# ScalarE's copy of the first row transform, placed ahead of two squares instead of behind them and a state part

## The reference

```python
x = x + _L0_conv_ref(_gn(x))      # DCT along both axes of every channel
x = x + _L1_conv_ref(_gn(x), ...) # six Euler steps of a small network
```

## Time and profile before

| what | value |
|---|---|
| median of 3 runs | 3459.21 us (3457.57 to 3469.12) |
| the profiled execution: its own time | 3467.75 us |
| its span in the profile | 3465.9 us, mean granted clock 0.935 |
| TensorE matmul (PE) busy | 3005.5 us, 87% of the span |
| TensorE weight load (PEld) busy | 2541.5 us, 73% |
| VectorE (DVE) busy | 2717.9 us, 78% |
| ScalarE (ACT) busy | 2440.3 us, 70% |
| GpSimd (POOL) busy | 875.2 us, 25% |
| DMA | 217.56 MB, mean 63 GB/s |

### The profile page before, as it was taken

The page is one execution under the profiler, slowest core; times in us unless marked ns, Lnnn a source line. Parts: engine busy times, 40 slices in busy tenths (PEclk is TensorE's granted clock), DMA queues, the critical chain, the costliest instruction groups (busy, mean ns, idle before and its releaser), DMA issues.

```text
span 3465.9 us, 148163 instructions
## 1 busy us (share of the span) xinstructions
PE 3005.5 (87%) x61684; PEld 2541.5 (73%) x61684; DVE 2717.9 (78%) x6273; ACT 2440.3 (70%) x3819; POOL 875.2 (25%) x1293
## 2 busy tenths in 40 slices
PE   3699988999889998899988999899988999888984
PEld 2578776777777787678767877777777777777873
DVE  6688876888868887788877888688886888768883
ACT  0377777677776777777776777777777767787774
POOL 3134311432123221223212331133311332111111
PEclk8799998999999999899999999999998999999997
DMA  3400033112231330322304213221133113131014
GB/s 84 89 22 22 25 55 96 49 49 80 37 96 49 91 72 4 96 77 69 68 18 112 66 49 68 59 87 49 50 67 96 49 49 92 25 95 59 31 49 112
DMA packets 370208, 217.56 MB, mean 63 GB/s; under 512 B 354544, under 2 KB 354912, under 8 KB 367456
## 3 DMA queue, kind: packets, MB, share of 16 engines
q1 hardware_dynamic: 369504, 207.64, 24.2%
HBM read 104.85 MB, written 77.07 MB: 52 GB/s over the span
## 4 chain that ended last, share of the span: by engine, by line
ACT 23%; PE 23%; issue 20%; DVE 20%; POOL 6%; DMA 3%; SPq 3%; DVEq 1%; POOLq 0%; ACTq 0%
PE cps L1482 16%; ACT z L714 8%; ACT z L682 6%; DVE y L1118 3%; PE sps L1597 3%; POOL m L562 3%; ACT unread_z L702 3%; PE tps L1588 3%; SPq L449 2%; DVE ha L1114 2%; DVE bnt L1144 2%; ACT hb L713 2%; ACT ha L713 2%; DVE hb L1114 2%; DMA y<-xa 2%
## 5 line engine op out<-in xcount | busy, mean ns | idle before, releaser
L1482 PE MATMUL cps<-ha,w 64*64 64x392 f16 (+1 forms) x27648 | 1418.8, 347 | 126.3 <-ACT z L682 75.4
L1482 PEld LDWEIGHTS cps<-ha,w 64*64 64x64 f16 x27648 | 1081.1, 110 | 332.0 <-issue 159.0
L1482 PE MATMUL cps<-hb,w 64*64 64x392 f16 x27648 | 1278.5, 334 | 20.8 <-issue 14.1
L1482 PEld LDWEIGHTS cps<-hb,w 64*64 64x64 f16 x27648 | 1091.7, 108 | 114.3 <-issue 25.9
L682 ACT ACTIVATE z<-cps,bias_now 128x784 f32<-128x784 f32 (+2 forms) x1056 | 759.1, 737 | 582.3 <-PE cps L1482 578.4
L519 POOL TENSOR_TENSOR small<-small,half 128x1 f32<-128x1 f32 x304 | 168.1, 553 | 1646.0 <-DVE small L1018 1008.4
L1114 DVE TENSOR_TENSOR ha<-z,ha 128x784 f16<-128x784 f32 (+2 forms) x384 | 385.0, 1003 | 150.4 <-ACT z L714 145.6
L1114 DVE TENSOR_TENSOR hb<-z,hb 128x784 f16<-128x784 f32 (+2 forms) x384 | 374.8, 976 | 86.6 <-ACT z L714 77.8
L1144 DVE BATCH_NORM_STATS2 bnt<-z 128x6 f32<-128x392 f32 (+1 forms) x768 | 385.8, 547 | 56.1 <-ACT z L682 55.7
L1118 DVE SCALAR_TENSOR_TENSOR y<-z,small,y 128x784 f32<-128x784 f32 (+2 forms) x384 | 396.4, 1035 | 0.1
L714 ACT ACTIVATE z<-z,small 128x784 f32<-128x784 f32 (+2 forms) x384 | 396.1, 1031 | 0.0
(11 more groups left out here) (161 smaller groups left out, 2650.9 us busy)
## 6 DMA issues: line engine op xcount, KB each, us to landing
xa<-x_dram SPq DMA_DIRECT2D x128, 196.0 KB, 5.1
y<-xa SPq DMA_DIRECT2D x16, 1568.0 KB, 7.6
y_dram<-y SPq DMA_DIRECT2D x128, 196.0 KB, 4.7
x_dram<-x1s SPq DMA_DIRECT2D x30, 784.0 KB, 6.0
fin<-y_dram SPq DMA_DIRECT2D x30, 784.0 KB, 7.5
xs<-in_x_dram SPq DMA_DIRECT2D x116, 196.0 KB, 4.5
fin<-x_dram SPq DMA_DIRECT2D x28, 784.0 KB, 5.7
out_dram<-fin SPq DMA_DIRECT2D x28, 784.0 KB, 3.6
```

The lines of the kernel that those rows point to most:

```text
L1482: return pe.matmul(dst, w[hin * 64:(hin + 1) * 64, kx, a, wl, :], src[:, :, 0:NA], start=(what == "X" and n == 0), stop=(what == "Y" and n ...
```

## The change

The copy of batch 0 moves up in ScalarE's order: from behind two squares and a state part to directly behind the fourth evacuation of phase 2. The helper that issues it is defined earlier so that it can be called there. Nothing else differs.

```diff
--- before
+++ after
@@ -756,6 +756,10 @@
                 def posted(what, slot):
                     return NPOST * (posts_before(g, s, kind) + POSTS[kind].index((what, slot)) + 1)
 
+                def copied(b):
+                    if kind == MID:
+                        batch_copy(b, NBATCH * hn + b, tps)
+
                 def final_state(slot, k):
 
                     act.wait_ge(yup_done, yup + NP * slot + 2 * k + 2)
@@ -817,6 +821,7 @@
                 squares(1, 1, c, sq + 5)
                 evacuate(1, 1, s, 2, 2, c)
                 evacuate(1, 1, s, 2, 3, c)
+                copied(0)
                 squares(1, 2, c, sq + 6)
                 squares(1, 3, c, sq + 7)
                 if kind == FIVE:
@@ -833,11 +838,6 @@
 
                 c = conv_at(g, s, 3)
 
-                def copied(b):
-                    if kind == MID:
-                        batch_copy(b, NBATCH * hn + b, tps)
-
-                copied(0)
                 copied(1)
                 evacuate(0, 0, s, 3, 0, c)
                 copied(2)
```

## The result

The changed kernel takes 3374.25 us (median of 4 runs, 3368.23 to 3376.15) against 3459.44 us (4 runs, 3457.57 to 3469.12). The ratio is 0.975, 95% interval 0.9733 to 0.9766. The profiled execution has a span of 3374.3 us and a mean granted clock of 0.952 (before: 3465.9 and 0.935).

The account below looks back on a forecast made before the run. TensorE was taken to bound the 28 MID steps (busy 62.03 of 66.23 us), its stalls being winnable. From the profiled 3467.75 us, 35 for waits and 56.4 for clock falls came off: 3376 us, range 3360 to 3433.

Parts of the forecast that it names:

- (a): Moved copy on ScalarE: row transform ends 0.63 us before the evacuation does (0.4 to 0.8 over steps), new wait 0.
- The slower rival: ScalarE stalls 2.4 us at the copy behind late rows at low clock; 3510 us, chance 0.06.
- (b): TensorE's stall for the copy removed: batch 1's rows start 2.40 us earlier.
- (d): Slot 1's statistics matmul next waits for VectorE's fourth product: 1.68 of 2.40 us left, new idle time 0.7 us.
- (c): ScalarE's squares and state part, queued behind the copy, each come later by its slot, 0.42 us.
- (e): VectorE's last split waits for the state part; L1062 reads statistics 0.9 us earlier; TensorE waits 0.1 for batch 0's `x1s`.
- (f): Second stall, batch 2's columns on `x1s`: grows from 1.05 to 1.4 us; step gains 1.25 us, 35 us over 28.
- (g): TensorE's clock falls behind the removed stall vanish, 16 long (3.04 us) and 5 short (1.55 us): 56.4 us.
- the clock's term: The 56.4 us forecast from TensorE no longer falling to 1.2 GHz behind the stall in MID steps.
- that of the waits: The 35 us forecast from shorter waiting, 28 MID steps at 1.25 us each.
- Rival 1: Two or three remaining idle times still bring TensorE's clock down; 3433 us, 3405 with half the falls, chance 0.18.

Follow-up runs that it names:

- the filled kernel: Against the kernel before: 12 matmuls with unread results put on TensorE in its 2.40 us wait for the copy in each MID step; 3413.5 us, ratio 0.9865.
- Half filling: Against the kernel before: 6 instead of 12 matmuls with unread results in TensorE's wait for the copy; 3422.3 us, ratio 0.9894.

## Why the prediction was right

It gave 3376 us (3360 to 3433), and 3374.25 was measured. By its steps:

- (a) No new wait at the copy: right; the rows end at 1544.74, ScalarE reaches the copy at 1545.50. The slower rival's mechanism, ScalarE waiting at the copy, exists and was made by placing the copy two evacuations earlier (where it also held up TensorE's X1); the margin of 0.4 to 0.8 us kept it away.
- (b), (d) The rows begin 2.4 us earlier and the statistics are held by the fourth product: right, with 0.87 us of idle time for the 0.7 forecast. The run with the copy behind the squares shows that this wait swallows 0.7 us.
- (c) The slot of the copy is 0.41 (0.42 forecast), and the split is late enough for VectorE to wait 0.48 us.
- (e), (f) 1.25 us per step forecast, 66.23 - 65.03 = 1.20 measured. The wait for `x1s` was to be 1.4 and is 1.36.
- (g) All 21 falls are gone, by the mechanism forecast, but the sum is closer than its terms. Between the profiled executions the span is 91.6 us shorter against 35 + 56.4 = 91.4. Filling the stall alone gave 52.4 there (3465.9 to 3413.5), and the rest is 39.2: the clock's term was 4 us too large and that of the waits 4 too small. One part of this shows in the filled kernel: with the falls gone, the first period of the groups 2 to 7 is held at 67.2 us by the wait for `xs`, so that a fall there gave back about 1 us less than was counted; most of that 1 us is won with the moved copy instead (65.03 us in five of the six). Between medians the sum is 85, since the profiled execution of before was 8.3 us slower than its median; there the filling gave 46. So the clock's term was about 10 us too large for a median run. That the errors cancel, and that 3376 lies within 2 us of the measurement, is luck.
- Rival 1 (the clock still falls) was nearer than its odds say. Half filling leaves 1.30 us and brings 2 short falls in 28; 1.62 us brings 7, 2.29 us 16, 2.40 us (before) 21, most of them long. The changed kernel's 1.36 us brings none. The sentence "1.4 is below what this trace shows to matter, but not by much" holds with the emphasis on the second half. The Trainium skill ("TensorE: Matmul & The Clock Gate", "A second HAM failure mode") tells of a kernel in which short idle times between matmul groups made the clock swing. Here stalls of 1.30 us and more agree with that in part of the steps, and the idle times of 0.87 and 1.36 us of the changed kernel do not.

The prediction took 1.7 us for the shortest single stall that a fall follows. Falls behind two shorter ones are missing from that. In the kernel before, 22 us ahead of the first copy of a group, TensorE stands still for 0.94 us ("issue": it waits for nothing that the profile shows), works for 0.6 and stands still again for 1.05. Then 45 matmuls take 3.83 us, where as many take 2.18 in X1, at a clock of 0.51:

```profile
2265.76 0.35 PE L1482 MATMUL cps<-hb,w 64*64 64x392 f16 x2 [0.94 <-issue]
...
2267.40 3.83 PE L1482 MATMUL cps<-hb,w 64*64 64x392 f16 x45 [1.05 <-ACT z L682]
```

```profile
2267.50:2271.00 3.50, 3.50 (x51) 2.65 (x54) 3.47 (x7) 1.85 (x6) 3.42 (x2) 0.51 0.02 5
```

A fall follows two idle times of at most 1.5 us at five of the six changes of group; at the sixth it is the 1.7. This suggests that idle time just before counts beside the length of one stall; the changed kernel's 0.87 and 1.36 us lie 10 us apart. No run tested such pairs by themselves.

## What to carry to other kernels

A wait of the engine that bounds a stage can cost twice, once as idle time and once as a lower TensorE clock after it: look at the granted clock behind each stall before pricing it, and try filling the stall with useless matmuls to see the two apart. A copy that frees a bank for TensorE belongs right behind the moment when its data are ready, in front of long work that nobody waits for yet, but not in front of an evacuation that TensorE needs sooner. After a stall is removed ask which input of the next instruction comes last, on all engines: here three kernels in a row were held next by VectorE's product, by another late copy, and by a transfer.

## What the runs showed of the hardware

Idle time and clock: in five kernels TensorE's longest stall in a MID step was 2.40 (2.25 in six of the steps), 2.29, 1.62, 1.36 and 1.30 us, and was followed by falls to 1.2 GHz in 21, 16, 7, 0 and 2 of 28 steps. I had expected a sharp limit and no difference between places. In two further kernels useless matmuls in the stall (0.31 or 0.21 us left idle) took all of these falls away, in two places. So 2 us more of matmul work per step, in 28 steps, made the kernel 46 us faster, as the theory had it. Two idle times of 0.94 and 1.05 us close together brought a fall as well, where one of 1.05 us by itself never did in the 28 MID steps.
